# A state-space scan on one NeuronCore: a plane addition moved from VectorE to an accumulating DMA, one more state buffer, and other moves between engines

## What is computed

```python
proj = hidden_states @ W_in.T
u, gate = jnp.split(proj, 2, axis=-1)
...
u = jax.nn.silu(jnp.transpose(x, (0, 2, 1)) + conv_b)
ssm_p = u @ Wx.T
...
delta = jax.nn.softplus(dt @ Wdt.T + dt_bias)

def step(state, xs):
    d_t, B_t, C_t, u_t = xs
    dA = jnp.exp(d_t[..., None] * A)
    state = dA * state + (d_t * u_t)[..., None] * B_t[:, None, :]
    y_t = jnp.einsum('bdn,bn->bd', state, C_t)
    return (state, y_t)
...
y = jnp.swapaxes(ys, 0, 1) + u * D_param
y = y * jax.nn.silu(gate)
return y @ W_out.T
```

## Time and profile before

| what | value |
|---|---|
| median of the runs | 2444.53 us |
| the profiled execution, its own time | 2442.7 us |
| its span | 2440.9 us |
| TensorE, mean granted clock | 0.962 of full speed |
| busy: PE, VectorE, GpSimd, ScalarE | 92%, 91%, 87%, 66% of the span |
| DMA moved | 352.15 MB, 144 GB/s on the mean |

### The profile page before, as it was taken

How to read it: one execution, slowest core, us unless ns; L and a number is a source line. 1 busy time by engine, 2 the same in 40 slices (tenths; PEclk the granted TensorE clock), 3 DMA queues, 4 the chain that set the end, 5 groups by cost and what they waited for, 6 DMA issues and landing times.

```text
span 2440.9 us, 30553 instructions
## 1 busy us (share of the span) xinstructions
PE 2240.2 (92%) x10140; PEld 1900.0 (78%) x10140; DVE 2229.0 (91%) x2104; ACT 1614.2 (66%) x3763; POOL 2116.4 (87%) x1090
## 2 busy tenths in 40 slices
PE   8989999999899998999989999999989977787879
PEld 7777878888678877888868887788878765666767
DVE  1389999999999999999999999999999999998892
ACT  1467667776777667776677667776677666765550
POOL 0189889999999999999899999999899999999870
PEclk9999999999999999999989998999999998989989
DMA  7454445444454444544455433644345332632342
GB/s 227 143 202 109 139 137 172 150 138 132 125 191 154 147 139 158 165 147 139 136 168 161 148 130 118 208 159 136 117 165 161 122 108 70 202 104 96 112 139 97
DMA packets 133178, 352.15 MB, mean 144 GB/s; under 512 B 38733, under 2 KB 43341, under 8 KB 131549
## 3 DMA queue, kind: packets, MB, share of 16 engines
q1 hardware_dynamic: 110254, 298.28, 37.9%
q10 hardware_dynamic: 22768, 51.93, 6.2%
HBM read 339.14 MB, written 11.02 MB: 143 GB/s over the span
## 4 chain that ended last, share of the span: by engine, by line
PE 42%; POOL 22%; DVE 21%; issue 9%; ACT 6%; DMA 1%; ACTq 0%; SPq 0%; DVEq 0%; POOLq 0%
POOL st L1530 12%; DVE scan L1303 11%; PE late L692 8%; PE ubank L638 7%; PE ubank L611 7%; POOL st L1538 6%; PE gbank L590 3%; DVE st L1315 3%; DVE ubank L1284 2%; PE scan L611 2%; DVE scan L1313 2%; ACT L1223 2%; POOL st L1544 2%; ACT scan L1133 2%; PE gbank L655 2%
## 5 line engine op out<-in xcount | busy, mean ns | idle before, releaser
L1530 POOL TENSOR_TENSOR st<-w_sb,bc 128x1024 f32<-128x1024 f32 x512 | 1198.0, 2357 | 122.7 <-PE gbank L655 110.3
L1303 DVE TENSOR_TENSOR_SCAN scan<-scan,st 128x1024 f32<-128x1024 f32 x512 | 1167.5, 2288 | 33.9 <-ACT scan L1133 18.4
L1133 ACT ACTIVATE scan<-delta,A_sb 128x255 f32<-128x255 f32 x2048 | 846.1, 459 | 0.1
L1538 POOL TENSOR_TENSOR st<-st 128x1024 f32<-128x1024 f32 x255 | 601.1, 2357 | 20.8 <-DVE st L1315 10.8
L611 PE MATMUL ubank<-h,wt 128*128 128x256 f32 x1712 | 423.3, 404 | 93.1 <-ACT qg L1223 87.6
L638 PE MATMUL ubank<-h,wt 128*128 128x256 f32 x2048 | 471.2, 384 | 23.2 <-ACT qg L1223 23.2
L611 PEld LDWEIGHTS ubank<-h,wt 128*128 128x128 f32 x1712 | 345.2, 204 | 161.8 <-ACT qg L1223 109.2
L638 PEld LDWEIGHTS ubank<-h,wt 128*128 128x128 f32 x2048 | 393.6, 193 | 81.7 <-ACT qg L1223 27.2
L1315 DVE TENSOR_TENSOR st<-scan,bc 128x1024 f32<-128x1024 f32 x384 | 453.8, 1208 | 0.0
L692 PE MATMUL late<-yg,wt 128*128 128x256 f32 x1792 | 407.1, 386 | 26.3 <-DVE x L1340 22.1
L1130 ACT ACTIVATE scan<-iota 128x4 f32<-128x4 f32 x512 | 86.9, 170 | 491.7 <-DVE st L1315 455.9
(11 more groups left out here) (219 smaller groups left out, 2257.1 us busy)
## 6 DMA issues: line engine op xcount, KB each, us to landing
wt<-in_W_in SPq DMA_DIRECT2D x256, 512.0 KB, 3.6
wt<-in_W_out SPq DMA_DIRECT2D x132, 512.0 KB, 3.4
wt<-in_cond_W SPq DMA_DIRECT2D x64, 512.0 KB, 3.6
bc<-bc_rows ACTq DMA_DIRECT2D x64, 512.0 KB, 6.8
wt<-G_tiles SPq DMA_DIRECT2D x32, 512.0 KB, 3.6
wt<-in_ffn_B SPq DMA_DIRECT2D x20, 512.0 KB, 3.6
xb<-in_x SPq DMA_DIRECT2D x8, 1024.0 KB, 7.1
x<-in_x ACTq DMA_DIRECT2D x28, 256.0 KB, 4.0
```

The costliest lines, as they stand in the source:

```text
L1133: last = fn(t[:, k, 1:T], delta[:, c, 1:T], ACT.Exp, scale=A_sb[:, col:col + 1])
L1303: v_.tensor_tensor_scan(Tps[q % 2][:, :], Tps[q % 2][:, :], x_, 0.0, ALU.mult, ALU.add).then_inc(scan_done, 1)
L1530: tt(st[:, n % ST_RING, :, :], w_sb[:, i % 2:i % 2 + 1, :].to_broadcast([P, NQ, T]), bc[:, 0, q * NQ:(q + 1) * NQ, :], ALU.mult).then_inc( ...
L1538: tt(st[:, n % ST_RING, :, :], st[:, n % ST_RING, :, :], st[:, (n - 1) % ST_RING, :, :], ALU.add).then_inc(add_done, 1)
```

## The change

The addition of planes 0 and 1 leaves DVE. The product of plane 1 is written to `st` like the others, and GpSimd issues a DMA (`add_dma`) that adds plane 0 to plane 1 within SBUF. GpSimd waits for its landing (`acc_st`) before its own addition of plane 2. DVE now multiplies each plane by C behind its own scan. `st` gets a seventh plane; the waits of `dbu` change with it. In softplus the ReLU on ACT and the addition on GpSimd are replaced by one DVE instruction (`delta_sum`) that reads the PSUM tile and ACT's logarithm, max(x,0) + ln(...), and writes `delta`. `sel` and `tmp` are gone from SBUF, and `wT` lies in `la`; `weights_b` uses two products of 64 columns with a broadcast column of the identity in place of one with `sel`.

```diff
-ST_RING = 6
+ST_RING = 7
...
             def weights_b(m, o):
-                return mm(o, sel[:, m * P:(m + 1) * P], wT[:, :], start=True, stop=True)
+                for e in range(2):
+                    pick = ident[0:E, 2 * m + e:2 * m + e + 1].to_broadcast([E, ER])
+                    last = mm(o[e * ER:(e + 1) * ER, :], pick, wT[:, :], start=True, stop=True)
+                return last
...
-            def dt_evac(job):
-                b, j = job[1], job[2]
+            def softplus(b, j):
+
                 n = 8 * b + j
-                act.wait_ge(*made(job))
-                if n >= 2:
-                    act.wait_ge(dadd_done, n - 1)
-                o = home(job)[:, :]
-                fn(delta[:, 2 * j:2 * j + 2, :].rearrange("p c t -> p (c t)"), o, ACT.Relu)
-                fn(tmp[:, j % 2, :, :].rearrange("p c t -> p (c t)"), o, ACT.Abs).then_inc(ev_inc(job), 1)
-
-            def softplus(b, j):
-                n = 8 * b + j
-                flat = tmp[:, j % 2, :, :].rearrange("p c t -> p (c t)")
-                act.wait_ge(*emptied(("dt", b, j)))
+                flat = delta[:, 2 * j:2 * j + 2, :].rearrange("p c t -> p (c t)")
+                act.wait_ge(*made(("dt", b, j)))
+                fn(flat, home(("dt", b, j))[:, :], ACT.Abs).then_inc(sp_step, 1)
+                act.wait_ge(sp_step, 3 * n + 1)
                 fn(flat, flat, ACT.Exp, scale=-1.0).then_inc(sp_step, 1)
-                act.wait_ge(sp_step, 2 * n + 1)
+                act.wait_ge(sp_step, 3 * n + 2)
                 fn(flat, flat, ACT.Ln, bias=1.0).then_inc(sp_step, 1)
...
+            def delta_sum(b, j):
+                job = ("dt", b, j)
+                n = 8 * b + j
+                d = delta[:, 2 * j:2 * j + 2, :].rearrange("p c t -> p (c t)")
+                dve.wait_ge(sp_step, 3 * n + 3)
+                v_.scalar_tensor_tensor(d, home(job)[:, :], 0.0, d, ALU.max, ALU.add).then_inc(delta_done, 1)
+                dve.wait_ge(delta_done, n + 1)
+                dve.sem_inc(ev_inc(job), 1)
...
-                if q == 1:
-                    v_.tensor_tensor(Tps[1][:, :], Tps[1][:, :], cq, ALU.mult).then_inc(prod_done, 1)
-                else:
-                    v_.tensor_tensor(plane(n), Tps[q % 2][:, :], cq, ALU.mult).then_inc(mul_done, 1)
-
-            def add_first(i):
-                dve.wait_ge(prod_done, i + 1)
-                dve.wait_ge(mul_done, 4 * i + 1)
-                v_.tensor_tensor(plane(4 * i + 1), Tps[1][:, :], plane(4 * i), ALU.add).then_inc(mul_done, 1)
+                v_.tensor_tensor(plane(n), Tps[q % 2][:, :], cq, ALU.mult).then_inc(mul_done, 1)
...
-                if q == 2 and i:
-                    pool.wait_ge(mul_done, 4 * i - 2)
-                if q == 1 and i >= 2:
+                if q == 2 and i >= 2:
                     pool.wait_ge(id_mm, i - 1)
+                if q == 3 and i:
+                    pool.wait_ge(acc_st[0], 16 * i)
...
+            def add_dma(i, k):
+                n = 4 * i + k
+                pool.wait_ge(mul_done, n + 1)
+                if k == 2:
+                    pool.wait_ge(acc_st[0], 16 * (i + 1))
+                pool.dma_start(st[:, n % ST_RING, :, :], st[:, (n - 1) % ST_RING, :, :], accum_op=ALU.add
+                               ).then_inc(acc_st[k - 1], 16)
+
             def add(i, k):
                 n = 4 * i + k
-                if k == 3:
+                if k == 2:
+                    pool.wait_ge(acc_st[0], 16 * (i + 1))
+                else:
                     pool.wait_ge(add_done, 3 * i + 1)
```

More of the change, by code:

```diff
@@ L219, in build @@
           A_mat, D_par, W_out, base_W, base_b, lora2_A, lora2_B, GT_all, ffn_B,
-          ident_in, mean_in, sel_in, iota_in, out):
+          ident_in, mean_in, iota_in, out):
     with ExitStack() as ctx:
@@ L278, in build @@
         sc = sb("sc", [P, 3, 2])
-        wT = sb("wT", [E, T])
+        wT = la[0:E, :]
         x2 = x2_flat[:, 0:KH * T].rearrange("p (k t) -> p k t", k=KH)
@@ L371, in build @@
         sp_step = sem("sp_step")
-        dadd_done = sem("dadd_done")
+        delta_done = sem("delta_done")
         dA_done = sem("dA_done")
@@ L376, in build @@
         scan_done = sem("scan_done")
-        prod_done = sem("prod_done")
         mul_done = sem("mul_done")
         add_done = sem("add_done")
+        acc_st = [sem(f"acc_st{i}") for i in range(2)]
         id_mm = sem("id_mm")
@@ L395, in build @@
         block = ctx.enter_context(nc.Block())
-        N_CONSTS = 12
+        N_CONSTS = 11
         SOFT_STEPS = 10
@@ L1084, in evac @@
                     act.wait_ge(*made(job))
+                    if b + 3 < B:
+                        act.wait_ge(*made(("cond", b + 3, 7)))
                     fn(wT[:, :], o[0:E, 0:T], ACT.Copy).then_inc(ev_inc(job), 1)
@@ L1123, in decay @@
                 if q == 0:
-                    act.wait_ge(dadd_done, 8 * b + c // 2 + 1)
+                    act.wait_ge(delta_done, 8 * b + c // 2 + 1)
                 if n >= 2:
@@ L1177, in _ @@
                     for prev in (late_job(i - 1), small_job(i - 1), end_job(i - 1)):
-                        if prev and prev[0] not in ("wout", "wb", "B", "lg", "ms"):
+                        if prev and prev[0] not in ("wout", "wb", "B", "lg", "ms", "dt"):
                             evac(prev, i)
@@ L1422, in _ @@
             norm(0)
+            delta_sum(0, 0)
+            delta_sum(0, 1)
             def take_late(i):
@@ L1448, in _ @@
                     soft_max_step(b - 1, 0)
+                mul(i, 0)
+                if weigh:
+                    soft_max_step(b - 1, 1)
                 scan(i, 1)
+                for n, j in softplus_of(i):
+                    delta_sum(n, j)
                 if i:
                     take_rest(i - 1)
-                if weigh:
-                    soft_max_step(b - 1, 1)
-                mul(i, 0)
                 if weigh:
@@ L1459, in _ @@
                     soft_max_step(b - 1, 3)
-                add_first(i)
+                scan(i, 2)
                 if weigh:
                     soft_max_step(b - 1, 4)
-                scan(i, 2)
-                if weigh:
-                    soft_max_step(b - 1, 5)
                 if i:
@@ L1469, in _ @@
                             conv_tap(v, k)
+                if weigh:
+                    soft_max_step(b - 1, 5)
+                mul(i, 2)
                 if c == 13 and b < LAST:
@@ L1472, in _ @@
                 scan(i, 3)
-                if i == CHUNKS - 1:
-                    y_sum(i - 1)
-                    y_gate(i - 1)
-                mul(i, 2)
                 if b and c == 10:
                     soft_max_in(b - 1)
-                mul(i, 3)
-                if i and i < CHUNKS - 1:
+                if i:
                     if i == NC - 1:
@@ L1487, in _ @@
                     y_gate(i - 1)
+                mul(i, 3)
             take_late(CHUNKS - 1)
@@ L1514, in weight @@
                 b, c = split(i)
-                pool.wait_ge(dadd_done, 8 * b + c // 2 + 1)
+                pool.wait_ge(delta_done, 8 * b + c // 2 + 1)
                 pool.wait_ge(u_done, i + 1)
@@ L1544, in fold @@
                 tt(t[:, 0:2, :], t[:, 0:2, :], t[:, 2:4, :], ALU.add).then_inc(add_done, 1)
-            def delta_add(b, j):
-                pool.wait_ge(sp_step, 2 * (8 * b + j) + 2)
-                tt(delta[:, 2 * j:2 * j + 2, :], delta[:, 2 * j:2 * j + 2, :], tmp[:, j % 2, :, :], ALU.add
-                   ).then_inc(dadd_done, 1)
-            delta_add(0, 0)
             weight(0)
-            dbu(0, 0)
-            delta_add(0, 1)
-            for q in range(1, Q):
+            for q in range(Q):
                 dbu(0, q)
             for i in range(CHUNKS):
-                for b, j in softplus_of(i - 1):
-                    delta_add(b, j)
-                if i + 1 < CHUNKS:
+                last = i + 1 == CHUNKS
+                if not last:
                     weight(i + 1)
-                    for q in range(3):
-                        dbu(i + 1, q)
+                    dbu(i + 1, 0)
+                add_dma(i, 1)
+                if not last:
+                    dbu(i + 1, 1)
+                    dbu(i + 1, 2)
                 add(i, 2)
-                if i + 1 < CHUNKS:
+                if not last:
                     add(i, 3)
```

10 lines of the change are left out of this document (1 added, 9 removed).

## The result

The changed kernel is slightly slower. Twenty runs give a median of 2454.11 us (2444.00 to 2471.16), twenty of the kernel before beside them 2444.49 (2440.09 to 2448.59): ratio 1.0040, 95% interval 1.0025 to 1.0055. The forecast was 2431 and faster; the range 2402 to 2530 holds the result.

The account below looks back on a forecast made before the run. PE was taken to bound c = 1 to 9, DVE c = 10 to 0, POOL batch 7. Batches 1 to 6 -12, batch 0 -3.5, batch 7 +2: -13.5 from 2442.7, 2429, as median 2431; range 2402 to 2530.

Parts of the forecast that it names:

- What L is: The passage estimating the new DMA's time from issue to landing: 3.6 us, plus 1.6, plus 0.5 for descriptors.
- L = 5.7: Forecast time in us from the new DMA's issue on GpSimd to its landing.
- x = the larger of d and L - 4.64: Addition to POOL's 16.10 us round: issue's hold on POOL, or landing time less two planes; forecast 1.1.
- the 1.6 for the accumulation: In the new DMA's landing: 1.6 us added because accumulating must read both source and destination.
- rival (c): Whole kernel: nothing moves, POOL's added time near 1.4 or PE swallows the gain; 2440 to 2449, chance 0.12.
- (b): POOL waits for the DMA's landing, so slower: from 6.0 us landing, 2529 at 6.8; chance 0.36.
- Rival (a): A quick DMA adds 0.33 to 0.9 us to POOL's round, DVE bounds c = 10 to 0; 2402 to 2404, chance 0.16.
- POOL rounds of 17.2, batch 7's slot from 16.14 to 17.2: Sign in GpSimd's loop: rounds of 17.2 us; batch 7's c = 8 reads the DMA's added time directly.
- the -12 of the sum: Slots c = 10 to 0 of batches 1 to 6: 121.6 in place of 123.6 us, -2.0 times six.
- Nothing either way: On DVE: plane 1's product becomes like the others, 1.208 us to SBUF, with no gain or loss.
- The new order's cover of 0.3 us: From the last tap ACT needs 5.3 us and DVE's work takes 5.6, so ACT's decay is covered by 0.3.
- Rival (d): The issue holds GpSimd until landing, or a port lock falls under it: round 21.8 us, near 2990; chance 0.03.

Follow-up runs that it names:

- the early version: The changed kernel with GpSimd's adding DMA issued one step earlier, before weight and the next chunk's first plane; 2404.07 us, ratio 0.983 to the kernel before.

## Why the prediction was wrong, point by point

**The step that failed** is the last one of "What L is": one middle value, L = 5.7, put into x = the larger of d and L - 4.64. The middle was right (measured median 5.6), and so was the 1.6 for the accumulation. The spread was left out: 4.4 to 8.8, with 45 of 128 above 6. I had written the ends down as bounds of one unknown value, and took x = 1.1 between them; short and long landings in fact alternate within one execution. The mean of a maximum is not the maximum at the median. A short landing gives nothing back, since x can't fall below the issue's cost; a long one is paid in full.

In numbers: the quiet round is 17.01, x = 0.91, below my 1.1. It is made of 0.61 from issue to the next plane and 0.3 by which two planes behind an issue are slower (4.95 against 4.64), and it lies inside the cover, which is therefore 4.64 + 0.91 = 5.55; the 8.8 of the landing at 1164.91, less the 3.25 waited, gives the same. So the formula itself holds: no wait below L = 5.55, and x = L - 4.64 above. To the 0.91 come 63.5 / 128 = 0.50 us of waits. So x = 1.41 on the mean in place of 1.1. The formula confirms it: applied to each of the 128 measured landings and averaged, with 0.91 for d, it gives 1.39; applied to their median alone it gives 0.95. By the forecast's own table x near 1.4 is rival (c), 2440 to 2449, and the edge of (b), "x = 1.4", is where slower begins. The profiled execution took 2448.0; the median of all, 2454.1, lies just above (c). Case (c) had a chance of 0.12, which was too little for the case that a spread about the middle leads to.

Rival (a) was priced well: with the cover long enough x is 0.9, and the time 2404 against its 2402 to 2404; c = 10 to 0 of batch 3 takes 118.39 against its "about 118.5". Its -30 for batches 1 to 6 came as -29.3. Its -7 and -4 for batches 0 and 7 came as +3.3 and -11.0, so that the total owes something to luck. What I called a quick DMA is in truth a well covered one. The forecast said that the wait for the landing was the thing and never asked whether the DMA stood at the right place in POOL's order, with nothing to pay for moving it.

- *POOL rounds of 17.2, batch 7's slot from 16.14 to 17.2:* 17.01, right to 0.2. Slots of 18 us, which I had named as proof against me, are there as well (17.98 and 18.01 at c = 2 and 6).
- *c = 1 to 9 of batch 3 unchanged:* 157.22, right. It holds less well in batches 1, 4 and 5, 158.2, 159.7 and 160.1 against 156.1, 158.6 and 157.5.
- *c = 10 to 0 at 121 to 122:* 123.82, wrong by the three late landings. This is the -12 of the sum; batches 1 to 6 came out at +7.1.
- *Landing at 5 to 6:* the median 5.6 is in, 45 of 128 are above 6.
- *DVE's load:* 93 us less, where the terms give 113. "Nothing either way" for plane 1's product was wrong: before, three products took 1.208 and the one that stayed in PSUM 1.220, and now all four take 1.219, 13.9 us more in all. The scans take 4.7 more. Also, c = 10 to 0 holds three `delta_sum` (c = 14, 15 and 0) and not four; over a batch the eight stand in c = 14, 15 and 0 to 5. In the early version DVE is busy for 116.53 us in these slots, against the forecast's 116.3, since these two errors nearly cancel. None of this is what failed.
- *delta_sum at 0.67:* 0.673 us, right. *Its waits covered:* right, ACT made DVE wait for 5.2 us in all.
- *The new order's cover of 0.3 us:* waits on decays 20.9 us, just above the 20 that I allowed, and 18.4 before; right as a mechanism. What the old order would wait for without add_first, 96.5 us, I did not see; it was readable from the earlier trace rows.
- *Batch 0:* -3.5 foretold, +3.2 from c = 2 on. The slot c = 6 takes 22.50 in place of 18.19. PE waits 2.17 us until the PSUM tile of softplus is free, which ACT used to release after |x| and DVE now releases after ln, and then y_sum, which stands ahead of a product, waits for PE's sum:

```profile
243.12 0.71 PE L737 MATMUL small<-x,wt 128*128 128x264 f32 x2 [2.17 <-DVEq L1294]
```

```profile
256.94 0.49 DVE L1319 SCALAR_TENSOR_TENSOR gbank<-u_sb,D_sb,gbank 128x256 f32<-128x256 f32 x1 [5.61 <-PE gbank L592]
```

  I had counted what `delta_sum` costs and waits for, and not how much longer it holds the tile. The two runs with the old order and `delta_sum` have 18.4 in this slot, the new order with the old softplus 18.66, so it takes both.
- *Batch 7:* +2 foretold, -6.0 measured. I had left out c = 10 to 12: 61.2 us before, 54.9 after. Batches 0 and 7 together were foretold at -1.5 and came at -2.8; that the two errors cancel is luck.
- *Rival (d), GpSimd held until the landing or locked out:* the issue takes 0.87, and the planes that do not follow an issue 2.35 beside a busy DVE. Nothing of it is seen.

On the Trainium skill: Collectives: The Full Stack, "The bandwidth ceiling" (two source reads, half the rate) is borne out in size by the 0.327 against 0.146 us a packet, a factor of 2.2; that it is the reads, no run shows. The fit of DMA: Bandwidth & Descriptors, "Anatomy of one DMA" gives 4.4 us with the bytes doubled, and 4.4 is the shortest landing measured; as an estimate of a typical landing beside 37% of other traffic it is 1.2 short of the median.
